# One layer of attention, experts and state-space mixing: the gate computed by one Silu activation, a weight split moved ahead of residual sums, and part of the stacked keys issued from GpSimd's queue

## What is computed

```python
x = x + attention(layernorm(x))      # 16 heads of 32, softmax over 1024 keys, masked
x = x + experts(layernorm(x))        # 8 experts of rank 16, top 2
x = x + mixer(layernorm(x))          # below
x = x + experts(layernorm(x))

# mixer, cut to what matters here
proj = u @ W_in.T
xBC, z, A_log = jnp.split(proj, [CONV_DIM, CONV_DIM + D_INNER], axis=-1)
xBC = causal_conv(xBC, conv_w) + conv_b           # 4 taps
y = state_space(xBC, A_log) + D[None, None, :, None] * x
out = y * jax.nn.silu(z + z_bias) @ W_out.T
```

## Time and profile before

| what | us |
| --- | --- |
| median of 3 runs | 3220.68 |
| lowest and highest | 3219.2 and 3228.18 |
| the profiled execution, its own time | 3233.71 |
| the profiled execution, its span | 3232.0 |
| PE busy with matmuls (share of the span) | 3028.8 (94%) |
| DVE busy | 2208.9 (68%) |
| ACT busy | 1090.6 (34%) |
| POOL busy | 755.5 (23%) |

### The profile page before, as it was taken

One profiled execution on the slowest core, in us unless ns is written; L12 is line 12 of the kernel. 1 busy time (PEld: TensorE's weight loads), 2 busy tenths in 40 slices (PEclk: granted clock), 3 DMA queues, 4 the chain that ended last, 5 costly groups with the idle time before them and its releaser, 6 DMA issues.

```text
span 3232.0 us, 59500 instructions
## 1 busy us (share of the span) xinstructions
PE 3028.8 (94%) x20772; PEld 2073.8 (64%) x20772; DVE 2208.9 (68%) x2975; ACT 1090.6 (34%) x1729; POOL 755.5 (23%) x1061
## 2 busy tenths in 40 slices
PE   3999999999999999999989999999998999999998
PEld 3654477777654447777765444777776554677776
DVE  2566587777755657777775666777766666787777
ACT  2133233434122323434312332434331333244342
POOL 3211112333121111233412110133321211123331
PEclk7899999999998899999999999999999999999999
DMA  9322111111221211111122220211122211021112
GB/s 335 83 50 61 28 51 48 44 51 49 75 65 47 46 40 43 45 51 44 50 73 66 69 49 14 59 48 44 44 70 74 59 46 46 26 63 44 52 45 76
DMA packets 163746, 191.55 MB, mean 59 GB/s; under 512 B 43962, under 2 KB 103994, under 8 KB 161786
## 3 DMA queue, kind: packets, MB, share of 16 engines
q1 hardware_dynamic: 157150, 175.83, 19.5%
q10 hardware_dynamic: 6432, 13.63, 1.3%
HBM read 106.99 MB, written 23.36 MB: 40 GB/s over the span
## 4 chain that ended last, share of the span: by engine, by line
PE 75%; DVE 11%; issue 4%; SPq 3%; DMA 3%; ACT 2%; POOL 1%; ACTq 0%; DVEq 0%; POOLq 0%
PE ps L728 14%; PE ps L730 12%; PE ps L729 12%; PE ps L880 7%; PE ps L843 6%; PE ps L863 5%; PE ps L1062 4%; PE ps L947 3%; PE ps L1048 2%; DVE LM L1669 2%; PE ps L1071 2%; PE ps L1108 2%; DMA KS<-EV 1%; DVE mneg L1575 1%; PE ps L738 1%
## 5 line engine op out<-in xcount | busy, mean ns | idle before, releaser
L728 PE MATMUL ps<-uh,win 128*128 128x512 f32 x1536 | 631.9, 411 | 4.2 <-POOL win L1824 3.4
L730 PE MATMUL ps<-uh,win 128*128 128x512 f32 x1536 | 605.4, 394 | 0.0
L729 PE MATMUL ps<-ul,win 128*128 128x512 f32 x1536 | 602.6, 392 | 0.0
L1575 DVE TENSOR_REDUCE mneg<-ps 128x1 f32<-128x128 f32 (+7 forms) x512 | 363.3, 753 | 155.8 <-PE ps L846 151.7
L1246 ACT ACTIVATE PR<-ps 128x1024 f32<-128x1024 f32 (+3 forms) x384 | 310.3, 810 | 419.0 <-PE ps L866 277.1
L880 PE MATMUL ps<-PR,VG 128*32 128x512 f32 (+3 forms) x1536 | 341.4, 521 | 12.7 <-DVE OS L1581 8.3
L728 PEld LDWEIGHTS ps<-uh,win 128*128 128x128 f32 x1536 | 291.7, 190 | 95.8 <-issue 29.6
L882 PE MATMUL ps<-PR,ones 128*32 128x512 f32 (+3 forms) x1536 | 341.4, 521 | 0.0
L1693 DVE TENSOR_TENSOR LM<-ps,LM 128x512 f32<-128x512 f32 x256 | 170.2, 686 | 244.7 <-PE ps L1062 197.1
L730 PEld LDWEIGHTS ps<-uh,win 128*128 128x128 f32 x1536 | 290.5, 189 | 66.2
L729 PEld LDWEIGHTS ps<-ul,win 128*128 128x128 f32 x1536 | 292.0, 190 | 55.0
(11 more groups left out here) (221 smaller groups left out, 5131.3 us busy)
## 6 DMA issues: line engine op xcount, KB each, us to landing
raw<-in_t SPq DMA_DIRECT2D x128, 256.0 KB, 2.8
QS<-EV SPq DMA_DIRECT2D x192, 128.0 KB, 2.4
KS<-EV SPq DMA_DIRECT2D x168, 128.0 KB, 2.4
in_t<-tiles ACTq DMA_DIRECT2D x10, 1024.0 KB, 9.5
XN<-in_L_attn_a_x_dram SPq DMA_DIRECT2D x40, 256.0 KB, 5.0
win_raw<-in_L_attn_a_Wqkv_dram SPq DMA_DIRECT2D x34, 256.0 KB, 3.2
win_raw<-in_t SPq DMA_DIRECT2D x32, 256.0 KB, 2.7
edec<-ed_t SPq DMA_DIRECT2D x512, 16.0 KB, 1.6
```

The source lines that it names most:

```text
L728: pe.matmul(dst, hi_l, hi_r, start=first, stop=False)
L729: pe.matmul(dst, hi_l, lo_r, start=False, stop=False)
L730: return pe.matmul(dst, lo_l, hi_r, start=False, stop=last)
L1575: dve.tensor_reduce(mneg[:, hh, t:t + 1], wide(b0)[:, 0:(t + 1) * P], AX.X, ALU.max, negate=True).then_inc(a_max.sem, 1)
```

## The change

The change has three parts, and two small ones.

1. A z tile is now one activation, `Silu` of the PSUM tile with bias `zb`, written to `zs`. The exponential, the addition of one, the reciprocal and the product are gone, and DVE has nothing of a z tile. PSUM banks are dealt out anew: z tiles always use bank 4 and 5, x tiles 0, 1 and 2, 3 in turn. The exponential of `edx` is moved in front of the activation of tile 2.
2. On POOL, the low half of group 1's weights is computed in front of the eight residual sums. The sums wait for one semaphore of all output stores.
3. The keys of head 0 of each pair are no longer issued by SP (or by ACT for the first pair) but by POOL (`first_keys`), with a semaphore of their own for each slot. SP issues queries of head 0, queries of head 1, keys of head 1.

```diff
-XZ_BANK = [0, 2, 4, 2, 0, 2, 4, 2]
+XZ_BANK = [4, 0, 4, 2, 4, 0, 4, 2]
...
             for hh in range(2):
                 j = 2 * hf + hh
                 for w in which:
+                    if w == 1 and hh == 0:
+                        continue
...
+        def first_keys(eng, hf):
+
+            for r, part in enumerate((0, 0, 1)):
+                eng.dma_start(KS[hf][r * HS:(r + 1) * HS, 0, :].bitcast(F32),
+                              EV[1][part][2 * hf * HS:(2 * hf + 1) * HS, :].bitcast(F32)).then_inc(s_keys[hf], 16)
...
                     if t == 0:
-                        pe.wait_ge(s_stack[slot][hh], occ * 96 + 96)
+                        pe.wait_ge(s_stack[slot][hh], (occ + 1) * (96 if hh else 48))
+                        if hh == 0:
+                            pe.wait_ge(s_keys[slot], occ * 48 + 48)
...
                 def turn_x(t):
 
-                    xz_dve.wait(pe, b, 2 * t + 2)
+                    xz_dve.wait(pe, b, t + 1)
...
-                    if t >= 3 and t != 2:
-
-                        xz_dve.wait(pe, b, t - 1 if t % 2 else t - 3)
+                    if t % 2 == 0 and t >= 2:
+                        xz_act.wait(pe, b, t - 1)
+                    elif t >= 5:
+                        xz_dve.wait(pe, b, (t - 3) // 2)
...
                 for t in range(2 * KT):
                     m = t // 2
+                    if t == 2:
+                        ed_in.wait(act, b, 1)
+                        act.activation(eds[:, :], edx[:, :], ACT.Exp).then_inc(ed_act.sem, 1)
                     xz_pe.wait(act, b, t + 1)
...
                     else:
-                        if t >= 2:
-                            xz_dve.wait(act, b, t - 1)
-                        act.activation(etmp, wide(XZ_BANK[t]), ACT.Exp, scale=-1.0, bias=nzb[:, m:m + 1]).then_inc(s_ze, 1)
-                        act.wait_ge(s_ze, b * KT + (m + 1))
-                        act.activation(etmp, etmp, ACT.Identity, bias=1.0).then_inc(xz_act.sem, 1)
+                        act.activation(zs[:, m, :], wide(XZ_BANK[t]), ACT.Silu, bias=zb[:, m:m + 1]).then_inc(xz_act.sem, 1)
...
-                for t in range(2 * KT):
-                    m = t // 2
-                    xz_act.wait(dve, b, t + 1)
-                    if t % 2:
-                        taps(xT[:, m, :], wide(XZ_BANK[t]), lambda k: conv[:, m, k:k + 1], ch, xz_dve)
-                        if t == 1:
-                            low_sums()
-                    else:
-                        ch.link(dve.reciprocal(etmp2, etmp))
-                        dve.scalar_tensor_tensor(zs[:, m, :], wide(XZ_BANK[t]), zb[:, m:m + 1], etmp2,
-                                                 ALU.add, ALU.mult).then_inc(xz_dve.sem, 1)
+                for m in range(KT):
+                    xz_act.wait(dve, b, 2 * m + 2)
+                    taps(xT[:, m, :], wide(XZ_BANK[2 * m + 1]), lambda k: conv[:, m, k:k + 1], ch, xz_dve)
+                    if m == 0:
+                        low_sums()
...
                 pool.wait_ge(s_kone, b * 2 + 1)
+                until(pj_lo, b * 4, 4)
+                first_keys(pool, 0)
...
+                until(st_pe, b * 8, 0)
+                first_keys(pool, 1)
...
                             if hf == 0 and not last:
                                 group_lo(b * 4 + g + 1)
                                 until(qkw_lo, b * 4 + g + 1, 1)
+                                if first:
+                                    residual()
                             for c in range(2):
+                                if c and not last:
+                                    if hf == 0:
+                                        until(pj_lo, b * 4 + g + 1, 4)
+                                    until(st_pe, p + 1, 0)
+                                    first_keys(pool, hf)
                                 until(o_rec, p, c + 1)
```

More of the change, by code:

```diff
@@ L225, in hybrid_layer @@
         s_x = [sem(f"s_x{t}") for t in range(TT)]
-        s_out = [sem(f"s_out{t}") for t in range(TT)]
+        s_out = sem("s_out")
         s_stats = sem("s_stats")
@@ L255, in hybrid_layer @@
         s_stack = [[sem(f"s_stack{i}_{hh}") for hh in range(2)] for i in range(2)]
+        s_keys = [sem(f"s_keys{i}") for i in range(2)]
         s_mrow = [sem(f"s_mrow{i}") for i in range(2)]
@@ L288, in hybrid_layer @@
         xz_act = signal("xz_act", 8)
-        xz_dve = signal("xz_dve", 8)
+        xz_dve = signal("xz_dve", 4)
         xt_pe = signal("xt_pe", KT)
@@ L537, in _ @@
             sp.wait_ge(s_pre_st, 16 * 3)
-            for t in range(TT):
-                sp.sem_inc(s_out[t], 16)
+            sp.sem_inc(s_out, TT * 16)
             for end in (False, True):
@@ L686, in _ @@
                         sp.dma_start(out[bass.ds(b, 1), t * P:(t + 1) * P, :].rearrange("a p d -> p (a d)"), X[:, t, :]
-                                     ).then_inc(s_out[t], 16)
-            for t in range(TT):
-                sp.wait_ge(s_out[t], NB * 16 + 16)
+                                     ).then_inc(s_out, 16)
+            sp.wait_ge(s_out, (NB + 1) * TT * 16)
             sp.wait_ge(s_wv, NB * 16 + 16)
@@ L723, in _ @@
             pe.wait_ge(s_pre_act, KT)
-            pe.wait_ge(s_pre_low, 3)
+            pe.wait_ge(s_pre_low, 2)
             def three(dst, hi_l, lo_l, hi_r, lo_r, first, last):
@@ L1000, in _ @@
                     xzw_lo.wait(pe, b, t + 1)
[L1001 removed]
+                    if t == 3:
                         al_dve.wait(pe, b, TT)
[L1003 to L1005 removed]
+                    if t % 2 == 0 and t >= 2:
+                        xz_act.wait(pe, b, t - 1)
+                    elif t >= 5:
+                        xz_dve.wait(pe, b, (t - 3) // 2)
                     for c in range(2):
@@ L1114, in _ @@
                         turn_x(KT - 1)
-                        xz_dve.wait(pe, b, 2 * KT)
                     for c in range(2):
@@ L1214, in project_hi @@
                             for hh in range(2):
-                                act.wait_ge(s_stack[i][hh], (b * 4 + g) * 96)
+                                act.wait_ge(s_stack[i][hh], (b * 4 + g) * (96 if hh else 48))
+                            act.wait_ge(s_keys[i], (b * 4 + g) * 48)
                     pj.wait(act, b * 4 + g, first_at(ch) if first else ch + 1)
@@ L1300, in _ @@
                         act.copy(cum2[:, :], ps[:, 7, 2 * P:4 * P]).then_inc(cm_act.sem, 1)
-                    elif t == 2:
-                        ed_in.wait(act, b, 1)
-                        act.activation(eds[:, :], edx[:, :], ACT.Exp).then_inc(ed_act.sem, 1)
-                        tokens_of_x(m - 1)
                     elif t >= 2 and t % 2 == 0:
@@ L1527, in _ @@
             dve.wait_ge(s_load, 16 * LOADS)
-            dve.tensor_scalar(nzb[:, :], zb[:, :], -1.0, None, ALU.mult).then_inc(s_pre_low, 1)
             dve.tensor_scalar(bz[:, ER:ZC], bz[:, ER:ZC], BONUS, None, ALU.add)
@@ L1859, in _, with residual @@
                 pool.sem_inc(s_tick, 1)
-                for t in range(TT):
-                    pool.wait_ge(s_out[t], b * 16 + 16)
+                until(st_pe, b * 8, 0)
+                first_keys(pool, 1)
+                def residual():
+                    pool.wait_ge(s_out, b * (TT * 16) + TT * 16)
                     pool.sem_inc(s_tick, 1)
-                    i = pool.tensor_tensor(X[:, t, :], XN[:, t, :], bob[:, :], ALU.add)
-                i.then_inc(s_bias, 1)
-                pool.wait_ge(s_bias, b + 1)
-                pool.sem_inc(s_tick, 1)
-                for last in (False, True):
-                    with (pool.Fori(0, GROUPS - 1) if not last else ExitStack()) as i_:
-                        g = GROUPS - 1 if last else i_
+                    for t in range(TT):
+                        i = pool.tensor_tensor(X[:, t, :], XN[:, t, :], bob[:, :], ALU.add)
+                    i.then_inc(s_bias, 1)
+                    pool.wait_ge(s_bias, b + 1)
+                    pool.sem_inc(s_tick, 1)
+                for which in range(3):
+                    first, last = which == 0, which == 2
+                    with (pool.Fori(1, GROUPS - 1) if which == 1 else ExitStack()) as i_:
+                        g = 0 if first else GROUPS - 1 if last else i_
                         for hf in range(2):
@@ L1874, in _ @@
                                 until(qkw_lo, b * 4 + g + 1, 1)
+                                if first:
+                                    residual()
                             for c in range(2):
+                                if c and not last:
[3 more added lines that the diff above has]
+                                    first_keys(pool, hf)
                                 until(o_rec, p, c + 1)
-                                dst = OT[hf * 64:(hf + 1) * 64, g, c * HB:(c + 1) * HB] if last else \
+                                dst = OT[hf * 64:(hf + 1) * 64, g, c * HB:(c + 1) * HB] if isinstance(g, int) else \
```

7 lines of the change are left out of this document (1 added, 6 removed).

## The result

The changed kernel takes **3314.35 us** (median of 4 runs, 3312.55 to 3319.34), the kernel before, run beside it, 3224.43 us: a ratio of 1.0261, with a 95% interval of 1.0237 to 1.0285. By the ratio the change costs 84 us (the two medians lie 90 us apart); 3201 was predicted, and the range ended at 3222. The profiled execution has a span of 3310.8 us against 3232.0.

The account below looks back on a forecast made before the run. PE, with matmuls in 94% of the span, was taken as the bound. The terms -21 - 4 + 5 = -20 us, against the profiled 3233.7 and carried over to the median of 3220.7, gave 3201 us; range 3174 to 3222.

Parts of the forecast that it names:

- part 3: First head's keys issued by POOL at each pair: claimed to lose 5 us in all.
- slot 0: Three changes of pair per batch where PE already waited for keys: 0.6 us won, 12 times, 7 us.
- G: Price of one DMA issue on POOL, taken as 1.0 us, between SP's 0.62 and a POOL memset's 1.80.
- Rival A: POOL issues keys as cheaply as SP, near 0.7 us each, winning 12 us there: 3180 us in all; chance 0.2.
- slot 1: Three changes of pair per batch without a wait before, POOL busy with a product: 0.4 us lost, 12 times, 5 us.
- first change: First change of pair in a batch, keys behind POOL's memset: 1.7 us lost, 4 times, 7 us.
- first pair: First pair of a batch, whose keys ACT issued before: claimed even.
- C: Theory of the experiments, not of the prediction: transfers of two queues at once slow each other.
- part 2: Weight split ahead of POOL's sums: 4 us won in batch 1, 3.04 of waiting and 1 for the clock.
- Rival B: Keys from POOL come late at each change of pair, deciding from G = 1.2: 3230 to 3277 us; chance 0.15.
- Part 1: Gate as one Silu in the x and z stage: wait for `edx` gone, 5.3 us per batch, 21 us in all.
- Rival C: The x and z stage keeps its length, set by the weight chain (DMA, ACT, POOL): 3214 us; chance 0.15.

Follow-up runs that it names:

- e6: Changed kernel, but SP sends the second head's transfers only after POOL's keys for the first head have landed: 3250.1 us, ratio 1.0047.
- e5: Changed kernel, but POOL issues the second head's keys and the first head's are back on SP: 3319.2 us, ratio 1.0265.
- e10: Changed kernel, first head's queries and keys each sent in two halves, keys on POOL's queue (ACT's for a batch's first pair): 3180.4 us, ratio 0.9829.
- e11: The same halves as e10, but all on SP's queue, first halves first, second head last: 3225.5 us, ratio 0.9967.
- e12: Kernel of e10 with POOL's memset of the row of ones put behind its issues for a batch's first change of pair: 3160.9 us, ratio 0.9779.
- e4: Kernel before, with the weight split ahead of the residual sums alone: 3217.2 us, ratio 0.9954.
- e8: Changed kernel, but POOL issues the first head's queries and keys, and SP holds the second head until they have landed: 3312.0 us, ratio 1.0240.
- e9: Kernel before with gate and weight split, SP's one queue sending both heads' queries ahead of the first head's keys: 3325.4 us, ratio 1.0288.
- e2: Kernel before, with the keys' move alone and one semaphore for the output stores: 3312.1 us, ratio 1.0238.

## Why the prediction was wrong

**The step that failed** is in part 3: "from the end of the third issue to PE's product is 1.76 us", a value of SP's queue taken over to POOL's, beside SP's "queries, issued by 179.91, are there at 181.7". It takes for granted that a transfer lands as fast with a second queue at work. In the changed kernel that span is 4.41 us, as the timeline of one change at slot 0 shows:

```profile
259.80 5.43 SPq L466 DMA_DIRECT2D QS<-EV  x6
260.44 1.52 POOL L473 DMA_DIRECT2D KS<-EV  x3 [1.49 <-PE ps L871]
265.27 1.97 SPq L466 DMA_DIRECT2D KS<-EV  x3
266.37 0.33 PE L848 MATMUL ps<-KS,QS 96*128 96x128 f32 x1 [2.44 <-DMA KS<-EV]
```

By its own terms, the forecast had 4.8 us from SP's first issue to the product at slot 0, and 6.57 were measured: +0.6 for POOL's later start ("POOL starts at 178.2, as SP did" was a misreading too), -1.5 for the issues, +2.65 for the landing.

I had asked what an issue costs, and the answer would have been kind: G is 0.49 us, not 1.0 (1.52 for three). By my own formula the keys would then have come 1.5 us earlier than forecast, and Rival A, 3180 us, would have been the case. But the issue was not the bound. The change moves SP's queries of the second head up by three places, into the time in which the keys pass, and 6 transfers became up to 9. I wrote of it "the 21 DMA issues that SP loses per batch only let head 1's keys go earlier, for which nobody waits", and costed it at nothing. With the second head held back (e6) 33 of the 52 us of added waiting go, and the loss falls from 84 us to 15, so most of the loss hangs on that sentence. The other 19 us of waiting stay: 8.7 at the first pairs, which e6 left as they were, 5.9 at slot 0 and 4.6 at the first changes, where POOL begins after SP. How the landing of 3.3 us that POOL's transfers keep there divides into the start of its queue and the sharing with SP's three isn't shown.

The Trainium skill has the rule behind it (DMA: Bandwidth & Descriptors, "Issuing engines are not separate DMA queues"): transfers of several issuing engines run on the same 16 engines and interleave, so that several issuers save only the time to issue. The runs agree: in e5 SP's own issues and landings stretch beside POOL's, in e6, with six transfers at a time, SP's land in 2.4 us again, and e10 against e11 shows the issue time saved (4.18 and 5.26 us to the first product). By that rule the direction could have been read beforehand, the size not; I had weighed another section of the same page.

By places, the four kinds of part 3, us of waiting in all:

| place | forecast | before | after |
| --- | --- | --- | --- |
| slot 0, 12 times | 0.7 each | 1.32 to 1.38 each | 29.2 in all, 2.36 to 2.54 each |
| slot 1, 12 times | 0.4 each | none | 18.7, 0.76 to 2.29 each |
| first change, 4 times | over 2 | 1.9 in two | 13.4, 1.06 to 4.42 each |
| first pair, 4 times | as before | 0.82 to 0.89 each | 12.1, 3.0 each |

The first change was read rightly (POOL's memset makes it late; e12 removes that). The first pair, called even, is a plain sign of C: its queries come from SP, and its keys now from POOL and ACT at once (POOL begins at 115.42 in batch 0, ACT at 114.77), and ACT's land in 5.0 us where they took 3.1.

**The second step**, that the sum takes waits at their own length. Of the 52 us of added waiting (21.4 to 73.3), 9 stand at the first pairs, just ahead of the attention windows, and 43 in them. There PE's idle time grew by 41.5, as it should, and the clock added 51.2. I had put 1 us on the clock in part 2, and nothing in part 3. The windows of one change of pair at slot 0 show the mechanism. The changed kernel ahead of its wait of 2.43 us, and from 2.65 us after PE's return (length, PE busy, granted clock, DMA share, GB/s):

```profile
188.00:191.90 3.90, 3.60 (x35) 1.00 0.70 137
197.00:200.00 3.00, 3.00 (x14) 0.50 0.05 11
```

The kernel before, from 2.4 us after its wait of 1.32 us at the same place:

```profile
186.00:189.00 3.00, 3.00 (x24) 1.00 0.28 66
```

So read for all twelve changes at slot 0 (3 to 6 us after the wait), the granted clock is 0.50 after every one in the changed kernel (waits of 2.36 to 2.54 us), and after 4 of 12 in the kernel before (1.32 to 1.38 us), with 1.00 ahead of each. The longer waits bring PE to its lower level.

The slope is off as well: "9.6 us for each tenth of G" is 32 places at 0.3 us, while the places costed with G are 28, which gives 8.4. At G = 1.0 it changes nothing.

**Rival B** had the direction, at 0.15, and mostly its sign (waits of over 1.5 us came at all twelve changes of slot 0 and 6 of 12 at slot 1), but for a wrong reason: it hung on G over 1.2, and its 3230 to 3277 us fall short of 3314.

**Part 1 was right**, nearly step by step: the wait for `edx` is gone; the wait at tile 3 for POOL's low half is 1.01 us, 1.0 was forecast; at tile 5 it is 1.48, not 0.7, and at tile 7 there is none, where 0.3 was forecast; the stage takes 56.63 us, between the forecast's 56 and 57, at a clock of 1.00. In the changed kernel's timeline of PE:

```profile
506.52 1.03 PE L1000 MATMUL ps<-ident,xT 128*128 128x128 f32 x8
508.56 0.50 PE L731 MATMUL ps<-uh,win 128*128 128x512 f32 x1 [1.01 <-POOL win L1818]
```

Over four batches it won 18.4 us of the forecast's 21. The table loads in the pair loop cost nothing visible: the stage of the 16 pairs takes 1116.8 us, before 1122.7. These are the loads, of the lines of ACT:

```profile
L1324 ACT ACT_TABLE_LOAD x28 | 35.9, 1283 | 0.5
```

No drain shows beside the loads: the one ahead of `dec` in batch 0 starts at 500.77, 0.02 us behind the activation before it, and `dec` follows at its end, at 502.06.

**Part 2** was right in kind: the 3.04 us wait is gone, and e4 measures -15 +- 11 us where 4 were forecast and 16 was the bound. What the prediction said of POOL beside DVE held too: the 96 issues on POOL took 0.49 to 0.76 us each, those of slot 0 while DVE ran its copy and its reciprocal. **Rival C** fell with the stage's length.

## What to carry to other kernels

Before moving a transfer to a second queue, look at the share of the DMA engines between issue and landing: here it was 0.9, the queue was not the bound, and a second one mixed later transfers into the ones that are waited for. Ask also when the new engine gets to its issues: POOL came to them later than SP, by 0.6 to 2.6 us, and e8 lost as much as the change with nothing of the second head ahead. Send less ahead of and in the awaited transfer, and only then spread the issues. And price a wait of PE in a dense stage like this one at about twice its length, since here the clock lost as much as the standing still, or more.

## What the runs showed of the hardware

- An issue costs 0.49 us on POOL, 0.59 on SP and 0.62 to 0.65 on ACT (medians), for the same 128 KB copy within SBUF. Beside a second busy queue SP's issues stretch: six take 5.43 us in the changed kernel and 3.68 in e9; the longest single one took 2.8 us (e2).
- Landing of such a copy: 2.4 us alone on SP, 2.4 to 3.0 alone on POOL, 3.1 to 5.0 with two or three queues at work (medians of each kernel).
- The granted clock over attention was 0.96 to 1.00 where PE hardly waited (e12) and 0.87 to 0.92 where it waited 0.3 to 3.6 us at each change of pair, some every 30 us (e9). At slot 0 it was 0.50, the lower level of 1.2 GHz, 3 to 6 us after all twelve waits of 2.4 to 2.5 us, and after 4 of 12 waits of 1.3 to 1.4 us. A product of 96x128 takes 0.33 us at the higher one and 0.47 at the lower.

Not tried: e10 or e12 without the gate or the split, the queue of ACT for the halves, and POOL's three issues made as early as SP's, which would part its late start from its landing.
